# Expert gates in a mixture-of-experts attention kernel: the two highest by an eight-highest and a position instruction, in two slots of the tile

## The reference

```
logits = normalize(h) @ normalize(sim) - sigmoid(gates)     # 16 per row; h = layernorm(x)
open   = logits > 0
if no expert of the row is open: open the two with the highest logits
rw     = softmax over the open experts of relu(logits)
q, k, v = sum over experts e of rw[e] * (h @ proj[e])        # 64 wide each
attn   = causal softmax(q k^T / 8) @ v
out    = x + sum over e of (rw[e] * attn) @ o_proj[e]
```

## Time and profile before

| | |
|---|---|
| timed runs | 1015.42 us median of 3 (1013.68 to 1015.49) |
| profiled execution | 1017.61 us, span 1015.8 us |
| PE busy | 931.0 us, 92% of the span |
| DVE busy | 652.9 us, 64% |
| ACT busy | 230.7 us, 23% |
| POOL busy | 252.8 us, 25% |
| mean granted clock of PE | 0.96 of full speed |

### The profile page before, as it was taken

How to read it: one execution, slowest core, us unless ns; L and a number is a source line. 1 busy time by engine, 2 the same in 40 slices (tenths; PEclk the granted TensorE clock), 3 DMA queues, 4 the chain that set the end, 5 groups by cost and what they waited for, 6 DMA issues and landing times.

```text
span 1015.8 us, 15976 instructions
## 1 busy us (share of the span) xinstructions
PE 931.0 (92%) x5000; PEld 843.6 (83%) x5000; DVE 652.9 (64%) x1875; ACT 230.7 (23%) x543; POOL 252.8 (25%) x408
## 2 busy tenths in 40 slices
PE   4777867999999999999999999999999999999987
PEld 3555545999989998988998899889999989898965
DVE  6788863766565657575666675757574757574742
ACT  6666750211111111111111111112021111111111
POOL 4544444513021302121212121202030212121201
PEclk9788876999999999999999999999999999999998
DMA  5445422110101010101010101010101010101010
GB/s 172 157 168 201 164 94 103 64 52 11 52 12 53 11 53 11 53 11 53 0 62 0 53 10 52 11 53 10 52 11 52 11 52 11 52 12 42 11 42 21
DMA packets 30574, 53.68 MB, mean 53 GB/s; under 512 B 7241, under 2 KB 7241, under 8 KB 30386
## 3 DMA queue, kind: packets, MB, share of 16 engines
q1 hardware_dynamic: 30514, 53.01, 15.2%
HBM read 36.22 MB, written 16.78 MB: 52 GB/s over the span
## 4 chain that ended last, share of the span: by engine, by line
issue 45%; PE 24%; POOL 8%; POOLq 4%; DVE 3%; ACT 0%; DVEq 0%
PE psQ L1265 15%; POOL mixedT_lo L957 7%; PE psO L1351 5%; POOLq L893 1%; POOLq L896 1%; PE psM L1338 1%; POOLq L898 1%; DVE rank L1080 1%; PE psT L1240 1%; POOLq L890 1%; PE psQ L1351 1%; POOL pow_tmp L889 0%; DVE mixed_f L1205 0%; POOL gates_q L952 0%; POOL pow_out L899 0%
## 5 line engine op out<-in xcount | busy, mean ns | idle before, releaser
L1265 PE MATMUL psQ<-Wqkv_hi,hT_hi 128*128 128x384 f32 (+1 forms) x1024 | 353.9, 346 | 8.4 <-DVE acc L1127 7.0
L1265 PE MATMUL psQ<-Wqkv_lo,hT_hi 128*128 128x384 f32 (+1 forms) x1024 | 347.1, 339 | 0.0
L1265 PE MATMUL psQ<-Wqkv_hi,hT_lo 128*128 128x384 f32 (+1 forms) x1024 | 346.8, 339 | 0.0
L1130 DVE SCALAR_TENSOR_TENSOR acc<-psQ,RW,acc 128x192 f32<-128x192 f32 x448 | 162.6, 410 | 229.8 <-PE psQ L1265 229.5
L1265 PEld LDWEIGHTS psQ<-Wqkv_hi,hT_hi 128*128 128x128 f32 x1024 | 193.1, 189 | 14.7 <-DVE acc L1127 11.2
L1265 PEld LDWEIGHTS psQ<-Wqkv_lo,hT_hi 128*128 128x128 f32 x1024 | 193.1, 189 | 1.6
L1265 PEld LDWEIGHTS psQ<-Wqkv_hi,hT_lo 128*128 128x128 f32 x1024 | 192.6, 188 | 0.0
L957 POOL TENSOR_TENSOR mixedT_lo<-mixed_f,mixedT_hi 128x512 fp32r<-128x512 f32 x64 | 82.6, 1302 | 203.6 <-ACT mixedT_hi L1025 203.6
L1351 PE MATMUL psO<-Wo_hi,mixedT_hi 128*128 128x512 f32 x248 | 99.2, 400 | 16.9 <-POOL mixedT_lo L957 16.9
L1351 PE MATMUL psO<-Wo_lo,mixedT_hi 128*128 128x512 f32 x248 | 97.9, 395 | 0.0
L1351 PE MATMUL psO<-Wo_hi,mixedT_lo 128*128 128x512 f32 x248 | 97.5, 393 | 0.0
(11 more groups left out here) (174 smaller groups left out, 1337.5 us busy)
## 6 DMA issues: line engine op xcount, KB each, us to landing
X<-in_x SPq DMA_DIRECT2D x8, 1024.0 KB, 5.5
x_scratch<-XR SPq DMA_DIRECT2D x16, 512.0 KB, 2.8
X<-x_scratch SPq DMA_DIRECT2D x32, 256.0 KB, 2.6
resid<-x_scratch SPq DMA_DIRECT2D x32, 256.0 KB, 3.1
out<-resid SPq DMA_DIRECT2D x32, 256.0 KB, 2.1
stage<-in_w_qkv SPq DMA_DIRECT2D x8, 768.0 KB, 6.2
mixed_f<-in_w_o SPq DMA_DIRECT2D x8, 256.0 KB, 3.1
CTX<-in_ctx_in SPq DMA_DIRECT2D x8, 154.0 KB
```

The costliest lines, as they stand in the source:

```text
L1130: dve.scalar_tensor_tensor(out=acc[e][:], in0=src, scalar=w, in1=acc[e][:], op0=ALU.mult, op1=ALU.add).then_inc(expert_added, 1)
L1265: last = pe.matmul(psQ[g % 4][:, 0:first_col(g) + PW], x[:, c * P:(c + 1) * P], w[:, c, E + g * PW - first_col(g):E + (g + 1) * PW], start ...
```

## The change

The gates are made by other instructions. `dve.max` writes the eight highest of the 16 logits in order (`top`), and `dve.max_index` where they stand (`top_at`). The exponential takes the logits themselves, with the highest as its bias, so that ACT needs only the first two instructions of the gates. `spare` gives the two positions a value that matches a column of `rev` only in a row without an open expert; two instructions add these to the weights. Before there were twenty DVE operations on the gates (the logits read among them) in slots 0, 1 and 2; now there are twelve, in slots 0 and 1. The slot in which ACT takes the exponential goes from 1 to 0, `gates_3` goes from slot 2 to slot 1, and the adds for slots 0 and 1 go there with it; 2 is then added in slot 2 and 3 in slot 3. The logits are followed by a `drain` in place of a wait.

```diff
STATS_SLOT, NORM_SLOT, H_T_SLOT = 1, 3, 5
-GATES_1_SLOT, GATES_2_SLOT, GATES_3_SLOT = 0, 1, 2
-ADD_AT = {0: (), 1: (), 2: (0, 1), 3: (2, 3), 4: (4,), 5: (5,), 6: (6,), 7: (7,)}
+GATES_1_SLOT, GATES_3_SLOT = 0, 1
+ADD_AT = {0: (), 1: (0, 1), 2: (2,), 3: (3,), 4: (4,), 5: (5,), 6: (6,), 7: (7,)}
...
             def gate(t):
                 act.wait_ge(gate_in_ready, t + 1)
-                act.activation(gate_exp[:], gate_in[:], ACT.Exp).then_inc(gate_exp_ready, 1)
+                act.activation(gate_exp[:], logit[:], ACT.Exp, bias=gate_bias[:, 0:1]).then_inc(gate_exp_ready, 1)
...
-                    if qkv and g == GATES_2_SLOT:
+                    if qkv and g == GATES_1_SLOT:
                         gate(t)
...
-                link(dve.scalar_tensor_tensor(out=logit[:], in0=psQ[0][:, 0:E], scalar=pow_out[p][:, 1:2],
-                                              in1=neg_sig[:], op0=ALU.mult, op1=ALU.add))
...
+                dve.scalar_tensor_tensor(out=logit[:], in0=psQ[0][:, 0:E], scalar=pow_out[p][:, 1:2],
+                                         in1=neg_sig[:], op0=ALU.mult, op1=ALU.add)
+                dve.drain()
+
+            def gates_1(t):
+
+                link(dve.max(top[:], logit[:]))
+                dve.tensor_scalar(gate_bias[:], top[:, 0:1], -1.0, 0.0, ALU.mult, ALU.min).then_inc(gate_in_ready, 1)
+                dve.max_index(top_at[:], top[:], logit[:])
+                link(dve.tensor_scalar(none_open[:], top[:, 0:1], 0.0, -1.0, ALU.is_le, ALU.mult))
+
+                link(dve.tensor_scalar(spare[:], top_at[:, 0:2], -float(E), none_open[:, 0:1], ALU.add, ALU.mult))
 
             def gates_3(t, j):
 
                 dve.wait_ge(gate_exp_ready, t + 1)
-                link(dve.tensor_tensor(chosen[:], chosen[:], gate_exp[:], ALU.mult))
-                link(dve.tensor_reduce(g1[:, 6:7], chosen[:], AX.X, ALU.add))
-                link(dve.reciprocal(g1[:, 7:8], g1[:, 6:7]))
+                link(dve.scalar_tensor_tensor(out=weight[:], in0=logit[:], scalar=0.0, in1=gate_exp[:],
+                                              op0=ALU.is_gt, op1=ALU.mult))
+                for n in range(2):
+                    link(dve.scalar_tensor_tensor(out=weight[:], in0=rev[:], scalar=spare[:, n:n + 1], in1=weight[:],
+                                                  op0=ALU.is_equal, op1=ALU.add))
+                link(dve.tensor_reduce(gate_sum[:], weight[:], AX.X, ALU.add))
+                link(dve.reciprocal(gate_inv[:], gate_sum[:]))
...
-                dve.tensor_scalar(RW[:, j, :], chosen[:], g1[:, 7:8], None, ALU.mult).then_inc(rw_ready, 1)
+                dve.tensor_scalar(RW[:, j, :], weight[:], gate_inv[:, 0:1], None, ALU.mult).then_inc(rw_ready, 1)
...
                         read_logits(t, tp)
-                        gates_1()
-                    if qkv and g == GATES_2_SLOT:
-                        gates_2(t)
+                        gates_1(t)
```

More of the change, by code:

```diff
@@ L22 @@
 U8 = mybir.dt.uint8
+U32 = mybir.dt.uint32
 P = 128
@@ L734, in experts_block @@
     logit = sb("logit", [P, E])
[L735 to L742, removed]
+    weight = sb("weight", [P, E])
+    gate_exp = sb("gate_exp", [P, E])
+    top = sb("top", [P, 8])
+    top_at = sb("top_at", [P, 8], U32)
+    spare = sb("spare", [P, 2])
+    gate_bias = sb("gate_bias", [P, 1])
+    none_open = sb("none_open", [P, 1])
+    gate_sum = sb("gate_sum", [P, 1])
+    gate_inv = sb("gate_inv", [P, 1])
     psQ = [ps(f"psQ{k}") for k in range(4)]
@@ L1357, in _ @@
             bodies(pe, body, [(moves, MOVES), (his, HIS)])
-OWN_STEPS = 4 * (7 + 4 + 3) + 4
+OWN_STEPS = 4 * (3 + 5) + 4
 _OUTS = [((8, 512, 512), 'float32')]
```

## The result

The changed kernel takes 1050.61 us, the median of 4 runs (1050.16 to 1055.21); the kernel before takes 1014.92 us with a fourth run (1013.68 to 1015.49). The ratio is 1.0364, 95% interval [1.0333, 1.0394]: 3.6% slower. The forecast was slower, 1034.3 us, with 1046 as the top of its range: the direction was right and the size was not. The profiled execution of the changed kernel is the longest of its four (1055.21 us), 4.6 us over their median. PE begins the experts' stage at 170.45 us in it, and in the kernel before at 168.12. From there to the end of the span it is 883.0 us instead of 847.7: +35.4 us in the stage that the change belongs to, so the loss lies there.

A forecast was written before the change was run, and what follows sets the result against it. PE, busy 92% of the span, was taken as the bound, so DVE savings count only through PE's waits. 15.4 - 1.0 - 7.0 + 11.5 made +18.9 us on 1015.42: 1034.3 us, range 1017 to 1046.

The forecast's parts named there:

- +15.4 for the tiles with the mix: Fourteen tiles: statistics end 1.10 us later on DVE, so PE's wait for `mixedT_lo` grows from 1.15 to 2.25 us.
- -1.0: Fifteenth wait for `mixedT_lo`, in the last batch: no statistics there, part 3 comes earlier, the wait goes; 1.0 us gained.
- -7.0: First tile of a batch: PE's five waits for the adds of slot 0 vanish, 7.0 us gained.
- +11.5 for the clock: Behind half of the fourteen longer PE waits the clock falls to 1.2 GHz, costing 1.65 us each; ends 0 and 23.1.
- Where the statistics end in the tile with the mix: Fourth tile of batch 2, on DVE: statistics end 8.9 us after the logits instead of 7.8, 1.10 us later.
- In 14 tiles: The delay worked out for the fourth tile of batch 2 was applied to fourteen tiles: +15.4 us.
- POOL's 5.38 us stand behind it as before: Mix tile: POOL's work between statistics and the end of `mixedT_lo` stays 5.38 us, so PE waits 2.25 us.
- All five waits go: First tile of a batch: adds of slot 0 come about 2.5 us earlier, PE needs 1.4; 7.0 us gained.
- at a new place: Sign of being wrong: PE waits somewhere new, as for the add of slot 1, now ahead of part 2; unpriced.
- the clock holds: Rival: PE's waits grow but the clock does not fall; sum +7.4 us, 1022.8 us, range 1018 to 1031; chance 0.22.
- Faster: Rival: with first `weight` and `spare` not held by POOL, mix tile statistics end 0.3 us earlier; 1003 us; chance 0.12.
- one hold gone: Rival that it cancels: only one of the `spare` and `weight` holds remains, sum -6 to +3 us; chance 0.06.

The follow-up runs named there:

- the run with PE filled: Changed kernel plus twelve matmuls of unread result on PE ahead of its wait for the last `mixedT_lo`, in k = 12 and 28: 1040.21 us, ratio 1.0251.
- the kernel with the adds back: Changed kernel with the adds for slots 0 and 1 back behind the statistics (old `ADD_AT`): 1012.25 us, ratio 0.9968.
- the exponential early and the adds back: Changed kernel with ACT's exponential ahead of part 1's `mixedT_hi` and the adds for slots 0 and 1 behind the statistics: 996.2 us, ratio 0.9792.
- the runs where the order stays the same: Includes the kernel before with the new gate instructions in its old order: 993.68 us, ratio 0.9785.
- the two kernels with one repair each: Changed kernel with only the adds for slots 0 and 1 behind the statistics, 1012.25 us, or only the exponential ahead of part 1's `mixedT_hi`, 1019.72 us.
- the kernel before with the statistics first: Kernel before, its old gate operations kept, with the next tile's statistics moved ahead of `gates_2` in slot 1: 1040.45 us, ratio 1.0237.
- the kernel with `spare` by column: Changed kernel with `spare` made by two instructions over one column each instead of one over two: 1036.81 us, ratio 1.0205.

## Why the prediction was right in its direction and too small

Its sum was +15.4 for the tiles with the mix, -1.0, -7.0 and +11.5 for the clock, +18.9 in all. Measured by the waits and by the run with PE filled: +22.9, -7.0, +7.1 and +10.4, which is +33.4 of the +35.7 us between the medians. The last 2.3 us are not assigned.

- **Where the statistics end in the tile with the mix: right in the tile that was read.** The prediction said 8.9 us after the logits instead of 7.8; it is 8.88. Its terms held one by one: `spare` held to the end of POOL's instruction; part 1 won by 1.13 us (447.10 - 445.15 = 1.95 instead of 3.08); from `mixed_f` to the end of the held `weight` 2.76 (said: 2.77); the adds 1.31 (said: 1.32).
- **"In 14 tiles": mis-sized, and the larger of the two errors.** The fourth tile of one batch stood for all. In the loop's five second tiles part 1 wins only 0.52 us, in part because DVE stands 0.65 us behind `spare`, and the statistics come 1.78 later; in the four tiles outside the loop they come 1.55 later (8.52 us after the logits instead of 6.97). Over the fourteen that is 20.4 us. The wait grew by 2.10 us in the five second tiles, by 1.51 to 1.52 in the loop's five fourth tiles and by 1.3 to 1.4 in the four outside the loop: 23.6 us, not 15.4. The fifteenth gave 0.7 back, not 1.0.
- **"POOL's 5.38 us stand behind it as before": wrong in the loop.** They are 5.73 in the tile that was read, mostly because one root step lasts 0.51 instead of 0.23 beside `H`. In the kernel before `H` came later, behind the add for slot 3, and that step was not held in any of its 32 instances (0.22 to 0.23); nor is it in the kernel with the adds back, where `H` is late again. From the end of the statistics to the end of `mixedT_lo` POOL takes 0.30 to 0.36 us more in the loop's ten tiles, and 0.15 to 0.26 less in the four outside it: 2.6 us in all. Of the 8.2 us by which the fourteen waits grew more than forecast, 5.0 are the statistics, 2.6 are POOL, and 0.6 is PE, which comes to the wait a little earlier. ("No gap" was not quite so either: within the 5.38 us POOL stands twice for 0.16.)
- **The first tile, -7.0: the wait went, the gain did not.** The step that failed is that "All five waits go" was booked as 7.0 us won, with nothing put in for the next wait in the same tile. I looked for what ended the wait that I removed, and not at what PE would reach next: the row maximum stood with no slack behind it, and the new order put the add for slot 2 in front of it. With the longer stand at the loop's turn this gave 7.1 us of new waits, which cancel the 7.0. The work taken away was smaller too: 2.2 us to the first add (3.70 instead of 5.89), not 2.5. The kernel before has nineteen gate operations and not twenty: DVE runs 192 instructions less in the changed kernel, six for each of the 32 tiles, where `max_index` is two of thirteen. The prediction named the place of its own error in general (PE waiting "at a new place"), and gave it no price.
- **The clock: the mechanism right, the size in part by luck.** Said: half of fourteen, 11.5 us. Half was a choice between two ends, for waits of 2.25 us; the waits became 2.11 to 3.16. Nine of fourteen fell in the profiled execution, and keeping PE busy gave back 10.4 us, 1.2 for each of nine instead of 1.65: two errors that nearly cancel.
- **The rivals.** That the clock holds was wrong, by the windows. "Faster" was named with its place, the first `weight` instruction. It does not hold in the kernel as changed, yet with the exponential early and the adds back it comes true at 996.2 us. Two ranges there don't follow from their terms: 3 to 14 falls make 1027.8 to 1045.9 us, not 1025 to 1048, and one hold gone makes -7.2 to +2.5 us, not -6 to +3; neither changes the outcome. The rule of the Trainium skill, VectorE: DVE Perf Modes, section Rules for kernel authors, that fewer chained operations are better, agrees with the runs where the order stays the same (0.9785); the change's own order is what turned it.
- **The holding.** The Trainium skill's rule in SBUF — State Buffer, section Who interferes with whom, which the prediction weighed, agrees with `spare` over two elements (0.81 us) and with `weight` (1.17). One-element instructions beside the same POOL instruction were not held (`none_open` 0.14, each half of `spare` 0.21 and 0.20).

## What to carry to other kernels

When a wait is taken away, look at the next instruction that the waiting engine would reach and at what releases it: a second wait can stand behind the first with no slack, and taking the first away only uncovers it. Separate an edit of the instructions from an edit of the order before you judge either: here the one alone gives 2% and the other alone costs 6.6%. And read more than one instance of the tile, one for each place in the loop and one outside it, before multiplying. Where an edit changes the number of instructions, look also at the packets that load the program: the time at the loop's turn went with them here.

## What the runs showed of the hardware

- A tensor_scalar over two elements per partition was held until POOL's 1.29 us instruction ended (0.81 us); over one element per partition it was not (0.14, 0.20, 0.21 us).
- The holding goes the other way too: a POOL tensor_scalar over one element per partition lasted 0.51 us beside DVE's `H` of 512 elements, and 0.23 us in all 32 instances of the kernel before, where `H` is not beside it.
- MAX8 over 16 elements took 0.18 us, MATCH_VALUE_LOAD 0.08 and FIND_INDEX8 0.17.
- Waits of equal length in the same code (2.66 us, and 3.15) were followed by the lower clock in some instances and not in others. In the two kernels with one repair each, whose waits at these fourteen places are 0.6 to 1.8 us, none was followed by it. Waits of that length are not free of it, though: in the kernel before with the statistics first two of PE's waits for the adds were followed by it (1.80 us ending at 507.2, 1.78 ending at 831.4), and in the kernel with `spare` by column one of 1.83 us.
- DVE stood 2.7 to 3.1 us at the loop's turn where two packets of instructions were loaded, and 1.8 to 2.1 us where it was one, at the four turns of each kernel here; that the one makes the other is not shown.
